# Loading two experts' weights in 32x32 blocks and turning them on VectorE, in a fused attention and mixture-of-experts layer

## The reference

```python
x = x + tanh(g_xattn) * attention(layernorm(x), ctx, ctx, mask, w_q, ..., w_o)   # x: 4 x 1024 x 256
xf = layernorm(x).reshape(4096, 256)
scores = softmax(xf @ gate_w.T)                 # 4 experts, the best 2 of each row
g = silu(einsum('nh,eih->eni', xf, eg))         # eg, eu: 4 x 688 x 256
u = einsum('nh,eih->eni', xf, eu)
y_exp = einsum('eni,ehi->enh', g * u, ed)       # ed: 4 x 256 x 688
y = einsum('enh,ne->nh', y_exp, comb)
y = y + silu(xf @ sg.T) * (xf @ su.T) @ sd.T    # the shared expert, for every row
x = x + tanh(g_ffn) * y
```

## Time and profile before

| what | us |
|---|---|
| median of 3 runs | 883.38 (883.05 to 883.73) |
| the profiled execution's own time | 881.68 |
| its span, first to last instruction | 879.9 |

### The profile page before, as it was taken

The page is one execution under the profiler, slowest core; times in us unless marked ns, Lnnn a source line. Parts: engine busy times, 40 slices in busy tenths (PEclk is TensorE's granted clock), DMA queues, the critical chain, the costliest instruction groups (busy, mean ns, idle before and its releaser), DMA issues.

```text
span 879.9 us, 19161 instructions
## 1 busy us (share of the span) xinstructions
PE 846.5 (96%) x6271; PEld 742.7 (84%) x6272; DVE 581.9 (66%) x1203; ACT 520.8 (59%) x1846; POOL 461.2 (52%) x551
## 2 busy tenths in 40 slices
PE   8788999999999999999999999999999999999995
PEld 7566788888888799999988888888888888889994
DVE  6899899999998577876564555555555545444442
ACT  4999999999999444656464444444445444322221
POOL 6686767667565353676531454444443444364442
PEclk9899999999999999999999999999999999999998
DMA  7125233322313222333240333222222232232221
GB/s 219 42 77 180 68 90 94 90 66 90 90 66 96 73 74 85 120 103 103 86 141 25 49 49 49 43 41 38 41 41 42 47 48 37 31 49 42 36 40 20
DMA packets 56887, 62.05 MB, mean 71 GB/s; under 512 B 15642, under 2 KB 45183, under 8 KB 56799
## 3 DMA queue, kind: packets, MB, share of 16 engines
q1 hardware_dynamic: 42871, 43.15, 15.8%
q0 software_dynamic: 12864, 17.57, 12.7%
q10 hardware_dynamic: 1064, 0.21, 0.1%
HBM read 34.78 MB, written 25.82 MB: 69 GB/s over the span
## 4 chain that ended last, share of the span: by engine, by line
PE 85%; ACT 5%; DVE 5%; issue 2%; DMA 1%; POOL 1%; DVEq 0%; SPq 0%; ACTq 0%; POOLq 0%
PE p_s L623 23%; PE p_f L640 12%; PE p_f L2767 9%; PE p_s L341 6%; PE p_f L2812 5%; PE p_s L2767 4%; ACT prob L1484 4%; PE p_t L2698 3%; PE p_t L352 3%; PE p_s L2684 3%; PE p_m L2725 3%; PE p_m L2665 2%; PE p_m L2713 2%; PE p_s L2812 2%; PE p_s L2870 1%
## 5 line engine op out<-in xcount | busy, mean ns | idle before, releaser
L509 POOL DMA_INDIRECT out_rows<-big_yout,slot_id x52 | 86.6, 1666 | 158.2 <-DVE big_yout L586 146.3
L1484 ACT ACTIVATE prob<-p_s,negmax 128x77 f32<-128x77 f32 x512 | 161.1, 372 | 7.2 <-DVE negmax L2032 7.0
L537 ACT ACTIVATE big_sil<-p_s 128x512 f32<-128x512 f32 (+1 forms) x78 | 46.6, 597 | 144.7 <-PE p_s L623 126.1
L1484 ACT ACTIVATION_READ_ACCUMULATOR prob<-p_s,negmax 128x1 f32 x512 | 128.9, 255 | 0.0
L569 DVE TENSOR_TENSOR big_hid<-p_s,big_sil 128x512 f32<-128x512 f32 (+1 forms) x78 | 54.0, 692 | 99.5 <-ACT big_sil L537 88.5
L623 PE MATMUL p_s<-big_fxT_hi,big_w_hi 128*128 128x512 f32 (+1 forms) x286 | 113.8, 398 | 0.3 <-ACT big_w_hi L529 0.3
L623 PE MATMUL p_s<-big_fxT_lo,big_w_hi 128*128 128x512 f32 (+1 forms) x286 | 112.7, 394 | 0.0
L623 PE MATMUL p_s<-big_fxT_hi,big_w_lo 128*128 128x512 f32 (+1 forms) x286 | 112.2, 392 | 0.0
L1108 POOL TENSOR_TENSOR prob<-prob,rinv 128x616 f32<-128x616 f32 x64 | 78.5, 1236 | 62.1 <-DVE rinv L2039 62.1
L1127 POOL TENSOR_TENSOR shT_lo<-shid,shT_hi 128x256 fp32r<-128x256 f32 x80 | 63.0, 800 | 44.4 <-ACT shT_hi L1526 44.3
L640 PE MATMUL p_f<-wd_hi,big_hT_hi 128*128 (+1 forms) x312 | 85.5, 280 | 0.0
(11 more groups left out here) (341 smaller groups left out, 2537.7 us busy)
## 6 DMA issues: line engine op xcount, KB each, us to landing
xr<-in_x SPq DMA_DIRECT2D x16, 256.0 KB, 2.9
x_scratch<-xr SPq DMA_DIRECT2D x16, 256.0 KB, 2.8
xn_scratch<-xn SPq DMA_DIRECT2D x16, 256.0 KB, 2.1
xt_scratch<-xnT SPq DMA_DIRECT2D x16, 256.0 KB, 3.2
xin<-xt_scratch SPq DMA_DIRECT2D x16, 256.0 KB, 3.6
x1in<-x_scratch SPq DMA_DIRECT2D x16, 256.0 KB, 3.3
out_rows<-syout SPq DMA_DIRECT2D x16, 256.0 KB, 2.2
raw<-in_L_ffn_ed SPq DMA_DIRECT2D x4, 688.0 KB, 4.3
```

Of the source, the lines that this page charges most:

```text
L509: pool.indirect_dma_start(out, bass.IndirectOffsetOnAxis(slot_id[:, column(j, t)], 0), yout[:, t, :], None, compute_op=ALU.add).then_inc(s ...
L1484: last = act.activation(prob[n % 2][t][:, m * PW + h * SK:m * PW + (h + 1) * SK], p_s[:, 2 * t + h // 4, col:col + SK], ACT.Exp, bias=negm ...
```

## The change

The matrices of experts 0 and 1 (q of 0 to 5) no longer go through TensorE. SP loads each in blocks of 32x32 so that the four groups of 32 partitions hold the columns that they shall have (`load_turned`): 12 DMAs for a gate or up matrix, 24 for a down matrix, with rows of 128 bytes. DVE turns every 32x32 block in place of a row of blocks, straight into the place of the low part: `flip(q, part)`, two parts for a matrix, of 672 and 32 columns for gate and up (the second waits for the first, as they overlap) and of 768 for down. ACT rounds it to the high part (`flip_hi`), now from SBUF, and DVE subtracts in place (`flip_lo`, "all of their low parts by VectorE"). The 22 groups `e_T`, `e_hi` and `e_lo` of experts 0 and 1 and their `tails` go. The `spread` steps, with `places`, `rows_at`, `shares_at`, `row_ids` and `low_shares`, stand earlier, `AFTER_UNIT` changes, and a raw buffer is free again when DVE has read it. Apart from that, the four last results of the big blocks are split around `x_lo(1)`.

```diff
+def load_turned(eng, v, raw, s_raw, q):
+    n, kind = q // 3, "gud"[q % 3]
+    src = v["e" + kind][n]
+    for a in range(P // TURN):
+        rows = raw[a * TURN:(a + 1) * TURN, :]
+        if kind == "d":
+            for c in range(FC):
+                at = c * P + a * TURN if c < FC - 1 else CUT + a % 2 * TURN
+                eng.dma_start(rows[:, c * H:(c + 1) * H].rearrange("p (b x) -> p b x", x=TURN),
+                              src[:, at:at + TURN].rearrange("(b r) x -> r b x", r=TURN)).then_inc(s_raw, 16)
+        else:
+            blocks = rows[:, 0:KC * SIDE].rearrange("p (k b x) -> p k b x", k=KC, x=TURN)
+            for k in range(KC):
...
+            def flip(q, part):
+                dve.wait_ge(s_raw[q % 2], raw_count(q))
+                dst = turned_part(q, part, 1).bitcast(fp32)
+                if q % 3 == 2:
+                    n = FC // 2 * H
+                    last = nc.vector.transpose(dst, raw[q % 2][:, part * n:(part + 1) * n])
+                else:
+                    at = part * SIDE
+                    nc.vector.transpose(dst[:, 0:WHOLE], raw[q % 2][:, at:at + WHOLE]).then_inc(s_flipped, 1)
+                    dve.wait_ge(s_flipped, 4 * (q // 3) + 2 * (q % 3) + part + 1)
+                    last = nc.vector.transpose(dst[:, FF - TURN:FF], raw[q % 2][:, at + WHOLE:at + SIDE])
+                last.then_inc(s_flip, 1)
+            def flip_lo(q, part):
+                dve.wait_ge(s_ehi, 2 * q + part + 1)
+                low = turned_part(q, part, 1)
+                nc.vector.tensor_tensor(low, low.bitcast(fp32), turned_part(q, part, 0),
+                                        ALU.subtract).then_inc(s_fliplo, 1)
...
+            def flip_hi(q, part):
+                act.wait_ge(s_flip, 2 * q + part + 1)
...
-        AFTER_UNIT = {2: 8, 3: 10, 4: 10, 5: 11, 6: 12, 7: 13, 8: 15, 9: 15, 10: 15, 11: 16}
+        AFTER_UNIT = {2: 8, 3: 9, 4: 11, 5: 12, 6: 13, 7: 14, 8: 15, 9: 15, 10: 15, 11: 16}
...
-                if q < 2:
...
+                elif q < 2 + 3 * FLIPS:
+                    sp.wait_ge(s_flip, 2 * (q - 1))
...
-                last_results()
+                last_results(0)
             if not last:
                 x_lo(j + 1)
+            if first:
+                last_results(1)
```

More of the change, by code:

```diff
@@ L906, in raw_count, with turned_part @@
         def raw_count(q):
[L908 removed]
+            return sum((384 if i % 3 == 2 else 192) if i < 3 * FLIPS else 16 if i % 3 == 2 else 32 for i in range(q + 1) if i % 2 == q % 2)
+        def turned_part(q, part, s):
+            e, kind = q // 3, "gud"[q % 3]
+            if kind == "d":
+                n = FC // 2
+                return ewd[s][:, e * FC + part * n:e * FC + (part + 1) * n, :].rearrange("p c h -> p (c h)")
+            o = 0 if kind == "g" else FF
+            return ewgu[s][:, e * KC + part, o:o + FF]
         def e_part(G, s):
@@ L2466, in late_units @@
                 inner(8, 0)
+                flip(0, 0)
                 inner(8, 1)
-                e_lo(0)
-                e_lo(1)
+                flip(0, 1)
                 chosen()
@@ L2474, in late_units @@
                 inner(8, 2)
-                e_lo(2)
+                flip(1, 0)
+                flip_lo(0, 0)
                 inner(8, 3)
@@ L2478, in late_units @@
                 inner(8, 4)
-                e_lo(3)
                 counts()
+                flip(1, 1)
                 inner(8, 5)
-                e_lo(4)
+                flip_lo(0, 1)
                 last_lo(8)
@@ L2493, in late_units @@
                 position(1)
-                e_lo(5)
+                flip_lo(1, 0)
                 inner(9, 4)
@@ L2497, in late_units @@
                 inner(9, 5)
-                e_lo(6)
+                places(0)
+                flip_lo(1, 1)
                 last_lo(9)
-                e_lo(7)
+                rows_at(0)
                 inner(10, 0)
+                flip(2, 0)
                 inner(10, 1)
-                places(0)
-                rows_at(0)
                 places(1)
+                flip(2, 1)
                 result(9)
-                e_lo(8)
                 inner(10, 2)
-                e_lo(9)
                 rows_at(1)
@@ L2512, in late_units @@
                 inner(10, 3)
-                e_lo(10)
+                flip_lo(2, 0)
                 inner(10, 4)
+                flip_lo(2, 1)
                 inner(10, 5)
+                last_lo(10)
                 places(2)
-                last_lo(10)
-                e_lo(11)
+                inner(11, 0)
                 rows_at(2)
-                experts_of_tiles()
-                inner(11, 0)
-                e_lo(12)
-                inner(11, 1)
-                result(10)
-                inner(11, 2)
@@ L2527, in late_units @@
-                e_lo(13)
-                inner(11, 3)
-                inner(11, 4)
-                inner(11, 5)
-                places(3)
-                last_lo(11)
-                e_lo(14)
-                rows_at(3)
-                inner(12, 0)
-                inner(12, 1)
-                places(4)
-                rows_at(4)
-                result(11)
-                inner(12, 2)
-                e_lo(15)
-                inner(12, 3)
-                e_lo(16)
-                e_lo(17)
@@ L2546, in late_units @@
-                inner(12, 4)
-                inner(12, 5)
-                last_lo(12)
-                e_lo(18)
-                places(5)
-                inner(13, 0)
-                e_lo(19)
-                inner(13, 1)
-                result(12)
-                rows_at(5)
-                places(6)
-                inner(13, 2)
-                rows_at(6)
+                inner(11, 1)
+                flip(3, 0)
+                result(10)
+                flip(3, 1)
+                inner(11, 2)
@@ new lines, in late_units @@
+                places(3)
+                inner(11, 3)
+                rows_at(3)
+                inner(11, 4)
+                flip_lo(3, 0)
+                inner(11, 5)
+                flip_lo(3, 1)
+                last_lo(11)
+                places(4)
+                inner(12, 0)
+                rows_at(4)
+                inner(12, 1)
+                flip(4, 0)
+                result(11)
+                flip(4, 1)
+                inner(12, 2)
+                flip_lo(4, 0)
+                inner(12, 3)
@@ L2560, in late_units @@
+                places(5)
+                inner(12, 4)
+                rows_at(5)
+                inner(12, 5)
+                flip_lo(4, 1)
+                last_lo(12)
+                places(6)
+                inner(13, 0)
+                rows_at(6)
+                inner(13, 1)
+                flip(5, 0)
+                result(12)
+                flip(5, 1)
+                inner(13, 2)
+                experts_of_tiles()
                 inner(13, 3)
+                places(7)
                 inner(13, 4)
+                rows_at(7)
@@ L2641, in _, with last_results @@
                     big_step(j, c)
-            def last_results():
-                for t in range(BT):
-                    big_result(NB - 1, t)
+            def last_results(pair):
+                for t in range(2):
+                    big_result(NB - 1, 2 * pair + t)
             late["vector"](dve, last_results)
```

190 lines of the change are left out of this document (86 added, 104 removed).

## The result

The changed kernel takes **896.04 us** (median of 4 runs, 893.59 to 896.57), the kernel before 883.56 us (4 runs, 883.05 to 884.04). The ratio is 1.0139 with a 95% interval of 1.0121 to 1.0158: some 12.5 us slower, where 883.0 was forecast with a range up to 888.5. The profiled execution took 895.96 us, with a span of 894.2 us and a mean granted clock of 0.985 (before: 881.68, 879.9, 0.992).

What follows compares the result with a forecast made beforehand. TensorE bounds the late units, DVE is the second bound and takes back what TensorE saves. 881.68 + 0.5 - 0.8 = 881.4 for the profiled execution, 1.7 us under the median, so 883.0; range 876 to 888.5.

Steps and rivals of the forecast that it cites:

- the walk through the late units: Units 8 to 14, step by step with the rows' durations: gate_up(14, 3) starts 0.5 us late.
- TensorE's 8.6 us of transposes: TensorE loses the transposes of experts 0 and 1, 8.6 us of the chain, 2.7 up to unit 9's end.
- The rival of twice that: On DVE float32 transposes take twice the ordinary time a column, each flip 0.7 to 0.8 us more: 888.8 us, chance 0.14.
- Units 8 and 9, `flip_hi(0, 0)` ahead of `gate(8, 1)`, `bases` 1.2 us, `down(8)`: In unit 8 ACT's flip_hi waits for DVE, delaying gate(8, 1); TensorE stands 1.2 us for bases, down(8) starts 2.3 us later.
- `down(9)` 1.9 us late: Unit 9: DVE catches up only while TensorE stands; down(9) starts at 359.25 in place of 357.34.
- The price of a block DMA, 0.43 us: On SP: a raw load's issue takes 0.43 us, so matrix 5's 24 DMAs end at 403.3.
- The clock as a rival at 0.10, worth 3 us once: After TensorE's waits at down(8) and down(9) the clock falls for some 6 us, costing up to 3 us: 886, chance 0.10.
- `flip_lo` 0.8 to 0.9 us, "ACT and POOL lose what they gain": On DVE each flip_lo takes 0.8 to 0.9 us; ACT and POOL lose their gains within 2 us a unit, under TensorE.
- 0.9 us before the spreads that end units 11 to 13: Units 11 to 13: TensorE waits 0.9 us in each for ACT's shares_at before the second spread.
- `last_results` -0.8 us: Second small tile: splitting last_results brings x_lo(1) sooner, so TensorE's 0.78 us wait goes, -0.8 us.
- `place_values` hidden: Step 4: despite SP's added issues place_values ends at about 97, landed by 100; prob_v started at 107.43, so hidden.
- The DMA rule: Block loads: below 512 bytes the engine reads, modifies and writes; by that alone, the time of four times the bytes.

Runs made afterwards that it cites:

- e9: The changed kernel with DVE's, ACT's, POOL's, SP's and TensorE's orders of units 8 to 14 written anew, same instructions; 883.23 us, ratio 1.0004 to the kernel before.
- e12: e9 with each flip_lo over 64 columns in place of 688 or 768, output another one; 876.75 us, ratio 0.9935 to the kernel before.
- e2: The changed kernel with matrices 0 to 5 loaded by 2 plain DMAs each, in place of 12 or 24 block DMAs, weights in wrong order; 892.57 us, ratio 1.0115.
- e1: The changed kernel with matrix 2's 24 block DMAs issued on SP behind store_y(7), load_x1(9) and load_rows(10), not ahead of them; 892.89 us, ratio 1.0129.
- e5: The changed kernel with 28, 34 and 16 identity transposes added on TensorE before down(8), down(9) and spread(7); 893.83 us, ratio 1.0126.
- e13: The changed kernel with the subtracted operand of flip_lo of matrices 0 to 4 read from PSUM, same columns, output another one; 891.82 us, ratio 1.0093.
- e6: The changed kernel with two swaps on POOL: h_lo(11, 4) ahead of low_shares(3), h_lo(12, 4) ahead of low_shares(5); 893.87 us, ratio 1.0120.
- e3: The changed kernel with each flip_lo over 64 columns in place of 688 or 768, output another one; 891.82 us, ratio 1.0095.

## Why the prediction was wrong

The forecast was 883.0 us with a range up to 888.5; it took 896.04. The step that failed is the walk through the late units: it ended 0.5 us late, and the change ended them 12.6 us late. Of the 12.1 us between, 4.6 are there at `down(9)`, and 7.5 come behind it. Term by term:

- **TensorE's 8.6 us of transposes**: nearly right. With the waits and the low stretch taken off, TensorE's lists of the late units are 8.1 us shorter in e9 and 8.2 in e12 than before.
- **The flips** (0.86 + 0.2, 0.9): right. The rival of twice that is refuted.
- **Units 8 and 9, `flip_hi(0, 0)` ahead of `gate(8, 1)`, `bases` 1.2 us, `down(8)`**: right. `bases` waited 0.72 us, and `down(8)` stood 3.70 us where the walk had 3.3. In e2, whose early part runs as before's, it starts at 345.07; the walk had 344.75.
- **`down(9)` 1.9 us late**: the first step that failed. It came 6.5 us late (8.2 less the 1.7 of the early part). The prediction priced the issues of matrices 0, 1 and 5 and said nothing of matrix 2's 24. What stands behind an issue on SP is late too: `load_rows(10)`, by 8.6 us (6.9 without the early part's 1.7). With the rows issued first (e1) `down(9)` is 4.0 us late, so the queue was 2.5 us of it; of the other 2.1 the low stretch behind `down(8)` is 1.5.
- **The price of a block DMA, 0.43 us**: 0.45 and gaps, 0.49 in all, for 24 of matrix 2, 0.57 for those of gate and up. Matrix 5's wait of 2 us came as forecast (2.09 us), though its issues began at 403.57 and not at 393.
- **The clock as a rival at 0.10, worth 3 us once**: the second failed step. It is no rival but a term. Each of the three forecast waits (3.3, 2.6 and 2.1 us in the walk; 3.70, 4.83 and 2.10 us in the trace) drew a low stretch in which TensorE lost 1.5 us. What that costs the kernel is less: filling all three waits (e5) gave 1 to 2 us.
- **`flip_lo` 0.8 to 0.9 us, "ACT and POOL lose what they gain"**: the third. `e_lo` had one operand in PSUM and `flip_lo` has both in SBUF, so it takes turns with POOL: 1.9 us more on DVE than in e13, 2.3 us more in POOL's 45 `h_lo` (951 for 899 ns), and `down(11)` and `down(12)` wait 3.2 us for POOL, on which the prediction had no wait at all. POOL's order has its part in these two waits (e6). e13 puts the price of the turns at about 4 us here; in e9 it is some 1.7 of the 6 us that `flip_lo` costs.
- **Behind `down(9)`**: the walk gave 1.4 us back there, the change lost 6.1 more. The 3.2 us for POOL and two low stretches, 3.0 us, are 6.2 of these 7.5; the last 1.3 us are not assigned.
- **0.9 us before the spreads that end units 11 to 13**: 0.62, 0.64 and 1.05. **`spread(7)` 2.1**: 2.10.
- **`last_results` -0.8 us**: failed. The wait went, and POOL's gather took its place.
- **`place_values` hidden**: right. Its issues ended at 103 where the walk had 97, and `prob_v` starts at 109.17 against 107.43, no later than the early part's 1.7 us.
- **The DMA rule**: a block DMA of 256 rows of 128 bytes landed 2.0 us after its issue (median of 48). SP issues one each 0.49 us, and that sets the rate: 688 KB in 11.7 + 2.0 us. The DMA queue while only these ran, from 336 to 347 us (packets, MB, share of 16 engines):

```profile
q1 hardware_dynamic: 5763, 0.70, 43.5%
```

That is 13.3 ns a packet of mostly 128 bytes, within the 10 to 20 ns that the prediction took. From 340 to 346 us before, the plain loads and stores moved 1.40 MB in 66.3% of the engines' time, so an estimate of 5.8 ns for 128 bytes: a byte costs 2.3 times as much in short rows. The Trainium skill (DMA: Bandwidth & Descriptors, Specifications) has reading, modifying and writing below 512 bytes. The trace agrees that short rows cost more, but not four times, which is what the prediction worked out from that rule.

Not separated: how much of e3's 4.2 us is DVE's time and how much POOL's turns (e13 gains as much with DVE's columns kept), and the single gains of e1, e5 and e6, each of 1 to 3 us with intervals that touch the changed kernel's.

## What to carry to other kernels

When an issue-heavy load is put on a queue, ask what stands behind it, not only when its data is needed. A wait of TensorE of over 2 us may bring a low stretch of the clock with it, 1.5 us here, and one of over 3 us did so each time; filling it with idle work is worth trying, though the kernel gets back less than TensorE does. Work moved from one engine to another is priced with the operands' memories: a two-operand instruction that had one of them in PSUM and now has both in SBUF can cost GpSimd its turn (`flip_lo` 1.00 us in place of 0.86, and waits of 3.2 us for GpSimd in place of 0.8). And the same instructions in another order were worth 12.5 us here, more than the transposes that the change removes.
